# Rounding, low parts and one up product moved in a hand-ordered two-layer kernel on one core

## The reference, cut to what matters

```python
# adapter, weights by language id
h = relu(x @ W1[lang] + b1[lang])                    # 512 -> 128
x1 = x + layernorm(x + h @ W2[lang] + b2[lang]) * gamma[lang] + beta[lang]
# perceptron, 512 -> 2048 -> 512 (384 shared columns, 128 of the expert)
g = gelu(x1 @ W1 + b1)
out = x1 + concat(g @ W2 + b2, g @ We[expert] + be[expert])
```

## Time and profile before

| what | value |
|---|---|
| median of 3 runs | 1453.47 us (1453.41 to 1453.83) |
| the profiled execution | 1455.1 us, its span 1453.3 us |
| PE busy | 1442.8 us (99%), granted clock at full speed in every slice |
| DVE, ACT, POOL busy | 949.9 (65%), 524.8 (36%), 652.7 (45%) us |
| chain that ended last | PE 90%, DVE 3%, POOL 3%, issue 2%, ACT 1% |

### The profile page before, as it was taken

One profiled execution on the slowest core, in us unless ns is written; L12 is line 12 of the kernel. 1 busy time (PEld: TensorE's weight loads), 2 busy tenths in 40 slices (PEclk: granted clock), 3 DMA queues, 4 the chain that ended last, 5 costly groups with the idle time before them and its releaser, 6 DMA issues.

```text
span 1453.3 us, 19122 instructions
## 1 busy us (share of the span) xinstructions
PE 1442.8 (99%) x6444; PEld 1185.0 (82%) x6444; DVE 949.9 (65%) x1596; ACT 524.8 (36%) x854; POOL 652.7 (45%) x640
## 2 busy tenths in 40 slices
PE   9999999999999999999999999999999999999999
PEld 5778888888888888888888888888888888888887
DVE  6899786775567756667557675577656676554444
ACT  4633454232433225232352333433234322432231
POOL 5996466441473514834138341384323743341101
PEclk9999999999999999999999999999999999999999
DMA  7857577553466545564455644646446454364332
GB/s 237 272 165 243 180 245 249 171 195 132 167 224 182 185 148 178 202 212 148 159 192 186 206 151 154 231 146 213 177 137 236 156 191 159 109 218 159 131 109 87
DMA packets 127764, 263.02 MB, mean 181 GB/s; under 512 B 12210, under 2 KB 84402, under 8 KB 119604
## 3 DMA queue, kind: packets, MB, share of 16 engines
q1 hardware_dynamic: 117876, 158.78, 34.3%
q10 hardware_dynamic: 9792, 103.03, 18.3%
HBM read 224.02 MB, written 37.75 MB: 180 GB/s over the span
## 4 chain that ended last, share of the span: by engine, by line
PE 90%; DVE 3%; POOL 3%; issue 2%; ACT 1%; ACTq 0%; DMA 0%; SPq 0%; DVEq 0%; POOLq 0%
PE down L255 15%; PE down L257 15%; PE down L256 15%; PE up_b L255 5%; PE up_b L257 5%; PE up_b L256 5%; PE up_c L257 3%; PE up_c L256 3%; PE up_c L255 3%; PE up_a L255 3%; PE up_a L256 3%; PE up_a L257 3%; DVE g L899 1%; POOL resid L1270 1%; PE aux L518 1%
## 5 line engine op out<-in xcount | busy, mean ns | idle before, releaser
L255 PE MATMUL down<-w,g 128*128 128x512 f32 x1024 | 401.1, 392 | 0.9 <-DVE g L899 0.9
L257 PE MATMUL down<-w,g 128*128 128x512 f32 x1024 | 398.6, 389 | 0.0
L256 PE MATMUL down<-w,g 128*128 128x512 f32 x1024 | 398.5, 389 | 0.0
L1277 POOL TENSOR_TENSOR w<-w_raw,ones 128x256 fp32r<-128x256 f32 x128 | 90.5, 707 | 616.2 <-DMA w_raw<-m_we 616.1
L255 PEld LDWEIGHTS down<-w,g 128*128 128x128 f32 x1024 | 192.3, 188 | 42.4 <-DVE g L899 3.2
L899 DVE TENSOR_TENSOR g<-g_raw,g 128x512 fp32r<-128x512 f32 x256 | 211.4, 842 | 23.1 <-ACT g L671 20.9
L257 PEld LDWEIGHTS down<-w,g 128*128 128x128 f32 x1024 | 192.2, 188 | 40.3
L256 PEld LDWEIGHTS down<-w,g 128*128 128x128 f32 x1024 | 192.3, 188 | 39.0
L663 ACT ACTIVATE g_raw<-up_a,m_b_sb 128x512 f32<-128x512 f32 x64 | 44.1, 690 | 407.7 <-PE up_a L257 383.0
L894 DVE TENSOR_TENSOR g_raw<-up_b,s 128x512 f32<-128x512 f32 x63 | 43.5, 691 | 222.0 <-PE up_b L257 178.3
L671 ACT CAST g<-g_raw 128x512 fp32r<-128x512 f32 x256 | 159.0, 621 | 8.1
(11 more groups left out here) (239 smaller groups left out, 2508.3 us busy)
## 6 DMA issues: line engine op xcount, KB each, us to landing
w<-w_kept ACTq DMA_DIRECT2D x55, 1792.0 KB, 7.6
w<-w_kept SPq DMA_DIRECT2D x56, 768.0 KB, 4.9
w_raw<-m_we SPq DMA_DIRECT2D x128, 128.0 KB, 4.6
out<-resid SPq DMA_DIRECT2D x64, 256.0 KB, 5.2
xTs_raw<-xT SPq DMA_DIRECT2D x56, 256.0 KB, 3.8
xs<-x SPq DMA_DIRECT2D x56, 256.0 KB, 4.9
w_kept<-w SPq DMA_DIRECT2D x8, 1792.0 KB, 7.7
aw_raw<-a_w SPq DMA_DIRECT2D x30, 256.0 KB, 4.5
```

Of the source, the lines that this page charges most:

```text
L255: eng.matmul(bank, a_hi, b_hi, start=opens, stop=False, skip_group_check=True)
L256: eng.matmul(bank, a_hi, b_lo, start=False, stop=False, skip_group_check=True)
L257: return eng.matmul(bank, a_lo, b_hi, start=False, stop=closes, skip_group_check=True)
L1277: eng.tensor_tensor(hi, values, ones[:, :, :].to_broadcast([P, 2, PART]), ALU.mult).then_inc(pool_eh[b], 1)
```

## The change

Six things move; no arithmetic of the result is added or left out.

1. The b2 row is rounded by GpSimd (`pool_b2_hi`, a multiplication with ones, ahead of its first square root) and no longer by ScalarE; one weight copy on ScalarE's queue moves behind its first ReLU.
2. In the first pair's opening ScalarE writes the high parts of B11 ahead of the kept copies, and B11's first chunk has the bank `down[3]`, so that TensorE puts six matmuls of C11 ahead of the low parts.
3. For k = 1 VectorE makes all 1792 low columns of `w1`; GpSimd's share is gone, and `keep_w1(1)` waits for VectorE alone. In the first pair ScalarE rounds T3 and an adapter weight earlier, T4 and `w1` of step 2 ahead of other work; GpSimd subtracts T3 ahead of the adapter weight, and splits the second batch's expert weights of step 0 only behind the sums of step 2 and T4.
4. In every later pair VectorE no longer makes the low parts of C12 and C22 of step k - 1 ahead of C21's: in steps 1, 2 and 3 they stand right behind `u2`, in steps 4 to 7 right ahead of the down sums (`dve_step`).
5. The first pair follows the same rule in steps 2 and 3 (`dve_second_step`, `dve_first_step`).
6. In the last step of the last pair P4 stands between the two halves of the down product of batch 0 (`pe_step`, `pe_down` with `halves`).

The 768 low columns are gone, and the second pair of expert rows moved behind the sums and T4. The diff, cut to its core:

```diff
-    FIRST_B11, FIRST_B21 = (up_a, down[1]), (down[2], down[1])
+    FIRST_B11, FIRST_B21 = (down[3], down[1]), (down[2], down[1])
...
                            stop=False, skip_group_check=True)
-        if k == 1:
-            eng.wait_ge(pool_w1, 3)
-        else:
-            eng.wait_ge(dve_w1, k)
+        eng.wait_ge(dve_w1, k)
...
         if i is first and k == 1:
-            eng.wait_ge(dve_w1, 1)
...
         cols = slice(b * PART, b * PART + D)
-        for h in range(2):
+        for h in halves:
...
                     last.then_inc(pe_y[b], 1)
-        if opens:
+        if opens and 1 in halves:
...
                 pe_down(eng, before(i), 1, GROUPS - 2)
+        elif i is last_pair and k == GROUPS - 1:
...
+            pe_down(eng, i, 0, k - 1, (0,))
+            pe_p4(eng, i, k)
+            pe_down(eng, i, 0, k - 1, (1,))
+            return
...
-    def act_first_part(eng, of, c, bank):
+    def act_first_hi(eng, of, c, bank):
...
         eng.wait_ge(pe_tr[0], b_count(first, of, c))
+        eng.copy(bo[:, of, c, HI, :], bank[:, :]).then_inc(act_bhi, 1)
...
+    def act_first_keep(eng, of, c, bank):
...
         eng.copy(kept, bank[:, :]).then_inc(act_kept, 1)
-        eng.copy(bo[:, of, c, HI, :], bank[:, :]).then_inc(act_bhi, 1)
...
         act_first_sum(eng, i, 1)
-        act_aw_hi(eng, m, 0, 0)
-        for c in range(2):
-            act_t_hi(eng, i, T3, c)
...
         act_g(eng, i, 1, C11)
+        act_t_hi(eng, i, T4, 0)
+        act_t_hi(eng, i, T4, 1)
...
         act_xT_hi(eng, m, 0, 3)
+        act_w1_hi(eng, 2)
+        act_g(eng, i, 1, C12)
         act_aw_hi(eng, m, 0, 1)
-        act_t_hi(eng, i, T4, 0)
-        act_t_hi(eng, i, T4, 1)
-        act_g(eng, i, 1, C12)
-        act_w1_hi(eng, 2)
...
-    def dve_rest_w1_lo(eng, k):
...
-        eng.wait_ge(act_w1hi, k)
-        eng.tensor_tensor(w1[:, k % 2, LO, A22:7, :], w1_raw[:, k % 2, LO, A22:7, :], raw(w1[:, k % 2, HI, A22:7, :]),
+    def dve_rest_w1_lo(eng):
...
+        eng.wait_ge(act_w1hi, GROUPS)
+        eng.tensor_tensor(w1[:, 0, LO, A22:7, :], w1_raw[:, 0, LO, A22:7, :], raw(w1[:, 0, HI, A22:7, :]),
...
         dve_g_lo(eng, i, 1, C21)
-        dve_g_lo(eng, i, 0, C22)
...
             dve_xT_lo(eng, m, b, c + 1)
-        if k > 2:
+        if k > 3:
...
             dve_sum_u2(eng, i, k)
-        else:
+        if k == 2:
+            dve_g_lo(eng, i, 0, C22)
+        if k == 3:
+            dve_g_lo(eng, i, k - 1, C12)
+            dve_g_lo(eng, i, k - 1, C22)
+        if k == GROUPS - 1:
...
             dve_sum_c21(eng, i, k - 1)
-            dve_g_lo(eng, i, k - 1, C12)
-            dve_g_lo(eng, i, k - 1, C22)
...
                 dve_t1(eng, m, 0)
+        if k > 3:
+            dve_g_lo(eng, i, k - 1, C12)
+            dve_g_lo(eng, i, k - 1, C22)
...
         dve_sum_u2(eng, i, k)
+        if k in (1, 2, 3):
+            dve_g_lo(eng, i, k - 1, C12)
+            dve_g_lo(eng, i, k - 1, C22)
...
+    def pool_b2_hi(eng):
...
+        eng.wait_ge(in_b2[0], 32)
+        eng.tensor_tensor(b2_row[:, HI, :], b2_row_raw[:, LO, :], ones[0:B2_ROWS, 0, :].to_broadcast([B2_ROWS, TOK]),
+                          ALU.mult).then_inc(pool_b2hi, 1)
...
         if n < 2:
-            slot, s = 0, slice(n * A22, n * A22 + 2)
+            s = slice(n * A22, n * A22 + 2)
...
         else:
-            slot, s = 3 - n, slice(A11, A22)
-            eng.wait_ge(act_w1hi, 1 if n == 2 else GROUPS)
-        eng.tensor_tensor(w1[:, slot, LO, s, :], w1_raw[:, slot, LO, s, :], raw(w1[:, slot, HI, s, :]),
+            s = slice(A11, A22)
+            eng.wait_ge(act_w1hi, GROUPS)
+        eng.tensor_tensor(w1[:, 0, LO, s, :], w1_raw[:, 0, LO, s, :], raw(w1[:, 0, HI, s, :]),
...
                     pool_t_lo(eng, i, of, c)
-            pool_first_w1_lo(eng, 2)
-            pool_aw_lo(eng, m, 0, 0)
...
             pool_t_lo(eng, i, T3, 1)
+            pool_aw_lo(eng, m, 0, 0)
             pool_expert(eng, i, 0, 1)
-            pool_expert(eng, i, 1, 0)
...
             pool_t_lo(eng, i, T4, 1)
+            pool_expert(eng, i, 1, 0)
...
         eng.wait_ge(dve_w1, k)
-        if k in (1, GROUPS):
-            eng.wait_ge(pool_w1, 3 if k == 1 else 4)
+        if k == GROUPS:
+            eng.wait_ge(pool_w1, 3)
...
             pe_first_down(eng, 1, 3)
+            eng.wait_ge(pool_w1, 2)
+            for c in range(2):
+                eng.wait_ge(act_bhi, b_count(first, B11, c))
+                first_hi(eng, C11, A11, B11, c, c == 0)
...
                 pe_first_low(eng, B11, c, FIRST_B11[c])
+            eng.wait_ge(act_bhi, b_count(first, B21, 0))
+            first_hi(eng, C11, A12, B21, 0, False)
             pe_first_low(eng, B21, 0, FIRST_B21[0])
-            pe_first_b12(eng, 0)
...
             pe_first_transpose(eng, B21, 1, FIRST_B21[1])
-            eng.wait_ge(pool_w1, 2)
-            first_half(eng, C11, A11, B11, True, False)
-            pe_first_low(eng, B21, 1, FIRST_B21[1])
+            for c in range(2):
+                first_lo(eng, C11, A11, B11, c, False)
+            pe_first_b12(eng, 0)
...
             first_half(eng, C21, A21, B11, True, False)
+            pe_first_low(eng, B21, 1, FIRST_B21[1])
...
                 pe_transpose(eng, first, 1, 2 + c, FIRST_B22[c])
+            first_hi(eng, C11, A12, B21, 1, False)
             eng.wait_ge(b_low, 4)
-            first_half(eng, C11, A12, B21, False, True)
+            for c in range(2):
+                first_lo(eng, C11, A12, B21, c, c == 1)
...
             load_b2_column(eng, language)
-            act_b2_hi(eng)
             load_b1(eng, first, 1, language)
+            act_relu(eng, first, 0)
             load_aw(eng, first, 1, 1, language)
-            act_relu(eng, first, 0)
...
             act_w2_hi(eng, 0)
-            act_first_part(eng, B11, 0, FIRST_B11[0])
-            act_first_part(eng, B11, 1, FIRST_B11[1])
-            act_first_part(eng, B21, 0, FIRST_B21[0])
+            for c in range(2):
+                act_first_hi(eng, B11, c, FIRST_B11[c])
+            for c in range(2):
+                act_first_keep(eng, B11, c, FIRST_B11[c])
+            act_first_hi(eng, B21, 0, FIRST_B21[0])
+            act_first_keep(eng, B21, 0, FIRST_B21[0])
...
             act_w2_hi(eng, 1)
-            act_first_part(eng, B21, 1, FIRST_B21[1])
+            act_first_hi(eng, B21, 1, FIRST_B21[1])
+            act_first_keep(eng, B21, 1, FIRST_B21[1])
...
                 act_xT_hi(eng, pairs[1], 0, c)
+            for c in range(2):
+                act_t_hi(eng, first, T3, c)
+            act_aw_hi(eng, pairs[1], 0, 0)
...
                 dve_t3(eng, first, c, FIRST_B22[c])
-            dve_rest_w1_lo(eng, 1)
+            dve_w1_lo(eng, 1)
...
                               base=0, pattern=[[-1, P]], channel_multiplier=1).then_inc(pool_minus, 1)
+            pool_b2_hi(eng)
...
```

More of the change, by code:

```diff
@@ L161, in build @@
     act_ready = sem("act_ready")
-    in_b2, act_ones, act_b2hi, dve_b2lo = sems("in_b2_", 2), sem("act_ones"), sem("act_b2hi"), sem("dve_b2lo")
+    in_b2, act_ones, pool_b2hi, dve_b2lo = sems("in_b2_", 2), sem("act_ones"), sem("pool_b2hi"), sem("dve_b2lo")
     pool_first_beta, dve_first_beta = sem("pool_first_beta"), sem("dve_first_beta")
@@ L338, in pe_p1 @@
         if i is pairs[1] and k == 0:
-            eng.wait_ge(pool_w1, 4)
+            eng.wait_ge(pool_w1, 3)
             eng.wait_ge(dve_w1, GROUPS)
@@ L406, in pe_p4, with pe_down @@
         up_product(eng, i, up_b, k, A22, T4, False, True).then_inc(pe_p[4], 1)
-    def pe_down(eng, pr, b, k):
+    def pe_down(eng, pr, b, k, halves=range(2)):
         opens, closes = k % 2 == 0, k % 2 == 1
@@ L697, in act_aw_hi @@
         eng.copy(tile[:, HI, :], values[:, LO, :]).then_inc(aw_rounded, 1)
-    def act_b2_hi(eng):
-        eng.wait_ge(in_b2[0], 32)
-        eng.copy(b2_row[:, HI, :], b2_row_raw[:, LO, :]).then_inc(act_b2hi, 1)
     def act_first_xb(eng, k):
@@ L955, in dve_b2_lo @@
         low = slice(LOW_ROW, B2_ROWS)
-        eng.wait_ge(act_b2hi, 1)
+        eng.wait_ge(pool_b2hi, 1)
         eng.tensor_tensor(b2_row[low, HI, :], b2_row_raw[low, LO, :], raw(b2_row[low, HI, :]),
@@ L1141, in dve_first_step @@
             return
-        dve_rest_w1_lo(eng, GROUPS)
+        dve_rest_w1_lo(eng)
         dve_w2_lo(eng, k)
@@ L1357, in pool_first_step @@
                 if n == 0:
-                    pool_first_w1_lo(eng, 3)
+                    pool_first_w1_lo(eng, 2)
                     pool_expert(eng, i, 0, k)
```

## The result

| | before | after |
|---|---|---|
| median, 6 runs each | 1453.41 us | 1461.71 us |
| single executions | 1452.15 to 1453.83 us | 1459.42 to 1468.39 us |
| profiled execution, its span | 1455.1, 1453.3 us | 1461.11, 1459.3 us |

The ratio is 1.0067, with a 95% interval of 1.0045 to 1.0089: slower, as forecast, but by 8.3 us where 2.8 were forecast, and above the range's end of 1460.5. The spread of the single executions is new: six lie within 1.7 us before and within 9 us after (longer series of the kernel before, of 27 to 29 executions, lie within 4.1 to 5.1 us). Ratios and intervals are those of executions at the usual clock; one execution of experiment 6, with a mean granted clock of 0.753, took 1804 us and stands outside them. The profiled execution of before is 1.7 us slower than its median, that of after 0.6 us faster, so the two spans differ by 6.0 us only.

The account below looks back on a forecast made before the run. TensorE was taken to bound the kernel. For the profiled execution 1455.1 - 3.7 (later pairs) - 1.7 (opening) - 0.5 (end) + 8.7 (step 1) = 1457.9 us; for the median 1453.5 + 2.8 = 1456.3 us, range 1450.5 to 1460.5.

Parts of the forecast that it names:

- The waits on `u2` and `g`: Later pairs, step 2: five waits on u2 and three on C21's low part go, a gain of 3.7 us.
- The new waits: Step 1: the aux product waits for VectorE's xTs, twice in the third, fifth and seventh pair; six pairs sum to 8.7 us.
- The long idle time ahead of the adapter weight: First pair: TensorE idle some 3 us ahead of GpSimd's adapter weight, which is done at about 76.7.
- step-1 term: Later pairs: two activation low parts ahead of the adapter input's make TensorE wait beside GpSimd's residuals, a loss of 8.7 us.
- the bounds of 0 and 16.8 us: Step-1 loss: nothing if GpSimd's residuals start late in every pair, 16.8 us if all start as in the third.
- the gains set against it, 5.9 us: All gains set against the step-1 loss: 3.7 us in later pairs, 1.7 in the opening, 0.5 at the end.
- opening's term: First pair: 1.2 us, capped by GpSimd's adapter weight, plus 0.47 for a wait on u2; 1.7 us gained.
- the b2 row on GpSimd: Opening: multiplication of 64x512 done within some 2 us, estimated at 2.1; TensorE's early wait goes, taken as 0.8 us.
- (a): Rival, chance 0.17: residuals start late in all pairs, step 1 loses 3 us in all instead of 8.7; 1450.6 us.
- (b): Rival, chance 0.10: TensorE doesn't wait in step 1 at all, all gains stay; 1447.6 us.
- (c): Rival, chance 0.10: GpSimd doesn't cap the opening, 3 us more are won; 1453.3 us.
- (d): Rival, chance 0.10: C12 late in step 2, 0.8 us in each of six pairs, 5 us more; 1461 us.

Follow-up runs that it names:

- experiment 6: Changed kernel with adapter low parts directly behind u2 and adapter-weight split ahead of bias rows, plus GpSimd's square roots ahead of expert splits in steps 3, 5, 7: 1452.44 us.
- Experiments 1, 2 and 4: Changed kernel with adapter low parts first (1453.1 us); part 4 undone (1454.13) or alone (1462.99); GpSimd's bias sums cut (1452.46), moved ahead of (1454.46) or between expert splits (1462.78).
- part 4 alone: Kernel before with only VectorE's new order in the later pairs: 1462.99 us, ratio 1.0067.
- part 4 with its order mended: Kernel before with part 4, but in step 1 the adapter input's low parts directly behind u2: 1451.55 us, ratio 0.9986.
- experiment 2: Two runs: changed kernel with VectorE's old order in the later pairs, 1454.13 us; kernel before with that new order alone, 1462.99 us.
- P4 alone: Kernel before with only P4 of the last step moved between the halves of the down product: 1453.99 us, ratio 1.0.
- the two without part 4: Changed kernel with VectorE's old order in the later pairs: 1454.13 us; the same with GpSimd's adapter-weight split ahead of its bias rows: 1453.26 us.
- experiment 3: GpSimd's adapter-weight split ahead of bias rows in the first pair: changed kernel 1461.3 us; with step 1's adapter low parts directly behind u2, 1451.06; without part 4, 1453.26.
- those of 5: Kernel before with part 4 and step 1's adapter low parts directly behind u2, 1451.55 us; kernel before with the move of P4 alone, 1453.99 us.
- experiment 1: Changed kernel with step 1's adapter-input low parts (chunks 2 and 3) directly behind u2, ahead of C12 and C22, in later pairs: 1453.1 us, ratio 0.999.
- the first run of experiment 3: Changed kernel with GpSimd's adapter-weight split ahead of its four bias rows in step 1 of the first pair: 1461.3 us, ratio 1.0051.

## Why the prediction was wrong, point by point

**Right: the mechanism and its place.** The waits on `u2` and `g` went and gave 3.6 us by the trace (3.7 forecast). The new waits are those of the `aux` product on `xTs` in step 1, twice in a pair where GpSimd's sums begin early; but these were the second and the fifth, where the third, the fifth and the seventh were forecast. That the waits of this profile, without the clock's part, sum to 8.3 us, near the 8.7, is luck: the second and the third pair traded places, and the seventh lost less. Experiments 1, 2 and 4 show it from three sides: the order, the part, the neighbour. The long idle time ahead of the adapter weight came where it was announced, 77.47 for 76.7.

**Wrong: the size of the step-1 term.** It was 8.7 us; between part 4 alone and part 4 with its order mended lie 1462.99 - 1451.55 = 11.4 us. Two things were wrong in it. I priced each pair by the one execution of before, "since the start follows from when a copy lands, and no copy is moved". But the landing differs in each execution: the second pair lost 2.3 us in one, 0.8 in another and 2.0 in a third, where I had 0, and the third pair 0.8, 2.0 and 2.1, where I had 2.8. The mean of the three sums is 11.5 us, close to the 11.4 of the medians; without the clock it is 10.0. That mix could not be read from one profile as a median, and the bounds of 0 and 16.8 us said so. And no term had the clock, although I had TensorE idle for some 3 us near 76.7 in my own forecast. It fell to half behind 1.67 and 0.72 us in the fifth pair, and behind 1.49 and 0.72 in the sixth pair of part 4 alone, and 1.5 and 1.6 us were added to 2.9 and 2.7. The Trainium skill ("TensorE: Matmul & The Clock Gate", Part 1) says that a gate passes fewer pulses to the array when it has been little busy; the trace agrees, with the 0.65 above. I had used that page nowhere, because the kernel before had no stretch below 1.00 to warn of it. The loss of 11.4 us is still inside the 3 to 13 that my range allowed; what put the total outside is that the gains set against it, 5.9 us, came to 1.6 (2.1 from part 4, and the 0.5 lost below).

**Wrong: the opening's term.** I forecast 1.7 us, capped by GpSimd's adapter weight. The cap was real, and its end moved by 0.5 us, not 1.2: the sums began at 52.04 (51.3 forecast), and the expert split behind them took 3.5 us, not 1.84, beside VectorE's low parts of `w1`. The bias sums behind that gave part of it back (6.85 us for 8.16 before).

```profile
57.09 3.09 DVE L1064 TENSOR_TENSOR w<-w_raw,w 128x1792 fp32r<-128x1792 f32 x1
```

```profile
52.04 0.74 POOL L1301 TENSOR_TENSOR w_raw<-a,w_raw 128x256 f32<-128x256 f32 x1 [1.90 <-DMA w_raw<-m_w]
...
58.26 2.39 POOL L1288 TENSOR_TENSOR w<-w_raw,ones 128x256 fp32r<-128x256 f32 x1
60.72 1.07 POOL L1290 TENSOR_TENSOR w<-w_raw,w 128x256 fp32r<-128x256 f32 x1
...
76.16 1.26 POOL L1234 TENSOR_TENSOR aw<-aw_raw,aw 128x512 fp32r<-128x512 f32 x1
```

In other executions even that was given back: in the profile without part 4 (experiment 2) the weight's product starts at 78.32, later than the 78.00 of the earlier trace rows, and the fall of the clock costs 1.6 us more. A lead that ends in a longer wait was booked as neutral; here it is a loss. By the medians opening and tail together are +0.5 us instead of -2.2, and not told apart from nothing. Of the smaller steps, the b2 row on GpSimd took 1.03 us (7.83 to 8.86), and TensorE's wait ahead of it went, as worked out.

**Wrong: trace against median.** I took gains read in an execution of 1455.1 as gains on the median of 1453.5. That execution held more waits than others: its pairs from the second to the seventh took 1070.5 us, those of three other profiles with VectorE's order of before (P4 alone and the two without part 4) 1069.1, 1068.5 and 1068.5. Part 4 mended took 1067.3, so it gives 3.2 us against that trace, but 2.1 on the median, where 3.7 were forecast.

**The rivals.** (a) and (b) fell with the eight waits, (c) with the wait at 77.47. Its other form, that the opening holds a gain once the cap is lifted, is true for about 1 us: 0.5 by the medians of experiment 3 against those of 5 (2.6 and 2.1 us ahead of before), 1.4 by those without part 4 (0.9 ahead, 0.5 behind). Neither difference is clear of the intervals. (d), C12 late in step 2, did not come; C12 is late by 0.1 us in step 5. A rival that was missing is that long waits slow TensorE behind them. By medians: 2.1 us gained, 11.4 lost, 0.5 lost elsewhere is +9.8 us; the change as a whole measured +8.3, and each of these differences is known to 1 or 2 us.

## What to carry to other kernels

When a step is put ahead of another on an engine, ask what the next one in the list feeds. Here two low parts for which nobody waits were put ahead of two that TensorE wants 3.3 us behind `u2`; turning the order (experiment 1) took the loss away. Price a wait that depends on a landing over several executions, not by the pattern of one profile, and read the spread of the runs as a sign of it. And let no engine arrive early at a cap: first lift the cap, then win the lead, since a long idle time of TensorE can be followed by microseconds at half its clock.

## What the runs showed that was not expected

The clock fell in profiles with an idle time of 2.8 us or more at one place of the opening (2.80, 3.36 and twice 4.09 us, with 1.5, 2.7, 1.6 and 1.6 us lost behind), but not with 2.86 in the changed kernel's own, nor with 2.27. In the pairs it fell behind 1.67 and 0.72 us, behind 1.49 and 0.72, and behind 1.81 and 0.72 in the first run of experiment 3, not behind 1.04 and 0.73. Nor did it fall in the seventh pair of that run, where the waits were within 0.03 us of the second of these cases:

```profile
1137.56 0.50 PE L255 MATMUL aux<-xTs,aw 128*128 128x512 f32 x1 [1.46 <-DVE xTs L921]
...
1139.25 0.50 PE L255 MATMUL aux<-xTs,aw 128*128 128x512 f32 x1 [0.71 <-DVE xTs L921]
```

So the length of the idle time doesn't settle it alone; what else does was not tried.

VectorE's low part of 128x512 took 0.60 to 0.68 us with GpSimd idle, 1.12 beside rows of 128x256 and 1.7 beside rows of 128x512, whose own length alone is 1.29 us. The Trainium skill ("SBUF — State Buffer", section "SBUF: two separate sides") has the port locked for a whole instruction, so that the partner's width is the price; the step with the width here (1.12 and 1.71) agrees with it.
